# Denominators, output bias, shift products and weight folds moved to other steps of an adaLN block

## The chip, the cores and the metric

One core of a Trainium2 chip runs the whole kernel. The metric is the device time of one execution in microseconds (us). The kernel before took 342.48 us, the median of three runs (341.78 to 342.52).

## The reference

The input x is (2, 2048, 256) fp32: 2 batches, 2048 tokens each. From a conditioning vector six modulation rows per batch are made. Two residual branches follow, first a linear attention with 16 heads of 16, then 8 experts of which each token uses two.

```python
mod = (silu(c) @ wmod).reshape(B, 6, 1, E)      # sa, ca, ga, sb, cb, gb
ga, gb = sign * maximum(abs, 0.25)
h = layernorm(x) * (1 + ca) + sa
Q, K, V = h @ Wq.T + bq, h @ Wk.T + bk, h @ Wv.T + bv
Q, K = elu(Q) + 1, elu(K) + 1                   # per head
KV = einsum('bshd,bshe->bhde', K, V); K_sum = K.sum(over tokens)
Z = 1 / (einsum('bshd,bhd->bsh', Q, K_sum) + 1e-6)
x = x + ga * (einsum('bshd,bhde,bsh->bshe', Q, KV, Z) @ Wo.T + bo)
h = layernorm(x) * (1 + cb) + sb
gates = top-2 softmax(h/|h| @ (c/|c|).T + h @ w_route.T)
x = x + gb * sum_e gates[e] * (gelu(h @ w1[e] + b1[e]) @ w2[e] + b2[e])
```

## The kernel before

**Tiling.** The 4096 tokens are 32 tiles of 128, taken in 16 units of two tiles; units 0 to 7 are batch 0 and 8 to 15 batch 1. x and Q stay in on-chip memory as `x_sb` and `q_sb`, 32 tiles each. fp32 products are made as three passes of fp32r: each operand is split into a rounded high part (`_hi`) and the rest (`_lo`), and high times high, high times low and low times high are added (`mm3`, L983 to L985).

**Two pipelines.** Every engine runs its own program, `step_a(u)` for the attention of unit u = 0 to 15 and then `step_e(u)` for the experts, u = -1 to 15; semaphores tie them together. The order of calls in each step, written out by hand, is the order of the work on that engine, and an engine waits at the first call that is not ready. In this text "step n" is `step_a` of unit n and "expert step n" is `step_e` of unit n.

- In step u TensorE projects the unit's two tiles (`qk`), transposes the next unit (`tp_a`) and adds the previous unit's x^T K into a bank (`xk`). ScalarE makes exp(min(q, 0)) (`negative_part`, `exp_qk`), casts the next unit's transposed tile and normalises the unit after that (`normalise`). VectorE makes the low part of the next unit, then Q and K (`feature_map`) and statistics of later units. GpSimd makes rstd (`make_rstd`) and low parts.
- In expert step u TensorE makes both expert products of unit u (`first`, `second`), the transpose of q*z of unit u+3 (`tp_o`), its attention (`attend`), and of unit u+2 the transpose (`tp_e`) and the router product (`route`). VectorE makes gates (`gates_a`, `gates_b`), multiplies by them (`gate`), modulates, adds the attention and scales the experts. GpSimd makes q*z (`make_qz`), router norms (`norm_e`), low parts (`lo_e`) and the last addition.

**Shift product.** The shift sa would have to be added to every normalised tile. For units 0 to 2 ("plain") it is. From unit 3 on the scale is folded into the weights: `fold(b, c)` on VectorE (L1392) makes chunk c of batch b's folded Q and K weights from the raw weights, and the last feature, which the layernorm makes redundant, is replaced by the shift's own row. That row is sa times the raw weights plus the bias, made by the two fp32 products at L1128 (`c_sum`, kept by `keep_c`), and is put into row 127 of chunk 1 by a DMA, `put_rows(b)` (L394), which SP issues. ScalarE rounds the folded chunks (`cast_folded`, L758), GpSimd makes the low parts (`low_folded`, L513). Unit 3 waits for both chunks of batch 0, unit 8 for batch 1. Before the change SP issues batch 0's row behind the loads of units 4 and 5, batch 1's row behind the value weights (`wv_sb`, L415), the casts are in steps 1 and 5, and chunk 0 is done first.

**Values.** `value_constants` (L1068) multiplies the shift by the value weights, and waits for their DMA. `fold_values` (L1410) scales these weights; `kv_of(0, .)` in step 10 reads them.

**Denominators.** `make_prod(u)` on GpSimd (L578) multiplies Q by the sum of K into the single buffer `prod`; `denominators(u)` on VectorE (L1553) reduces it and takes the reciprocal z. `make_prod` of a unit waits until the denominators of the unit before are made. z of the first `Z_AHEAD` units goes to slots of their own (5 before), later ones share one. Units 0 to 4 are done in steps 10 to 15, unit u+5 in expert step u. The product of unit 5 is placed on GpSimd between `make_qz` and `lo_gates` of expert step 0, its denominator at the end of that step on VectorE.

**Output bias.** `add_bo(u)` on GpSimd (L528) adds ga*bo to x of unit u, in the steps of `BO_STEPS` for the first units (6 of them), and in expert step u-5 for the rest. `add_attention(u)` waits for it.

Of the kernel before, what the change touches and what calls it, by code (L numbers as in the profile page):

```python
# [57 lines left out]
BO_STEPS = (6, 8, 8, 10, 14, 15)  # L58

def adaln_block(nc, x, wqkvT, rows, cols, woT, w1, w2, b2, cT, wmod, out):  # L60
# [13 lines left out]
    with ctx:  # L74
# [50 lines left out]
        Z_AHEAD = 5  # L125
# [28 lines left out]
        gate_sign, gate_abs, gate_size = (q_sb[0:64, 8 + k, :] for k in range(3))  # L154
# [60 lines left out]
        folded = [q_sb[:, 4:4 + NC * 2, :].rearrange("p (c k) e -> p c (k e)", c=NC), tr_f.rearrange("p h c n -> p h (c n)")]  # L215
# [149 lines left out]
        def _(sp):  # L365
# [28 lines left out]
            def put_rows(b):  # L394

                sp.wait_ge(c_kept, 1)
                sp.wait_ge(folded_made, NC * (b + 1))
                sp.dma_start(folded[b][P - 1:P, 1, :], c_sum[b:b + 1, :]).then_inc(d_fold[b], 16)

            for it in range(2, NU // 2):  # L400
                load_x(it, 0)
                load_x(it, 1)
                if it == 2:
                    put_rows(0)
# [11 lines left out]
            put_rows(1)  # L416
# [45 lines left out]
        def _(pool):  # L462
# [50 lines left out]
            def low_folded(b, c):  # L513

                pool.wait_ge(fold_hi, NC * b + c + 1)
# [19 lines left out]
            def step_a(u):  # L535
# [8 lines left out]
                if u.nth(1):  # L544
                    for c in range(NC):
                        low_folded(0, c)
                if u.nth(5):
                    for c in range(NC):
                        low_folded(1, c)
                if weights_ahead(u):  # L550
                    split_weights_lo(u.count(1, -2))
                if u.plus(-3):
                    split_weights_lo(u.count())
                if u.nth(UPB + 2):
# [8 lines left out]
                if any(u.nth(j) for j in range(UPB + 4, UPB + 7)):  # L563
                    make_prod(u.plus(-2 - UPB))
                for k, at in enumerate(BO_STEPS):
# [12 lines left out]
            def make_prod(u):  # L578

                if u.nth(5):  # L580
# [55 lines left out]
            def lo_gates(u):  # L636
# [5 lines left out]
                if u.plus(4) and u.plus(-1):  # L642
# [7 lines left out]
            def step_e(u):  # L650
# [12 lines left out]
                if u.plus(5) and u:  # L663
# [4 lines left out]
                if u and not u.nth(0) and not any(u.nth(j) for j in range(UPB + 3, NU)):  # L668
# [27 lines left out]
        def _(act):  # L696
# [60 lines left out]

            def cast_folded(b, c):  # L758

                act.wait_ge(folded_made, NC * b + c + 1)  # L760
# [77 lines left out]
            def step_a(u):  # L838
# [9 lines left out]
                exp_qk(u, 0)  # L848
                if u.nth(NU - 1):
# [10 lines left out]
                if u.nth(1):  # L860
                    for c in range(NC):
# [3 lines left out]
                if u.nth(5):  # L865
                    for c in range(NC):
                        cast_folded(1, c)
                if u.nth(6):
                    scale_last_value_row()
# [976 lines left out]
```

## Time and profile before

| what | value |
|---|---|
| median of the runs | 342.48 us (341.78 to 342.52) |
| the profiled execution | 342.43 us |
| its span, first to last instruction | 340.7 us |
| TensorE matmul busy | 329.8 us, 97% of the span |
| TensorE weight load busy | 307.3 us, 90% |
| VectorE | 277.8 us, 82% |
| GpSimd | 235.2 us, 69% |
| ScalarE | 224.7 us, 66% |
| mean granted TensorE clock | 0.994 of 2.4 GHz |

Times in the trace are microseconds from the first instruction. PE is TensorE, DVE VectorE, ACT ScalarE, POOL GpSimd, SP SyncE; a "q" behind an engine's name marks its issuing of DMAs, and "bank" is an accumulation bank. A row "[1.09 <-ACT x L740]" means that the engine was idle for 1.09 us before this work, and that the result written at line 740 by ScalarE ended the wait. The attention steps run from about 9 to 103 us, the expert steps from there to the end, one about every 14.2 us once they are in their rhythm. A row with a colon in front, as 34.00:49.00, is a stretch: its length, then busy us (and instructions) of PE, PEld (the weight load), DVE, ACT and POOL, the granted clock, the DMA engines' busy share and GB/s. Matmuls overlap in the pipeline, so a matmul's own duration is longer than the distance to the next.

### The profile page before, as it was taken

The page shows a single profiled execution, that of the slowest core. Times are in us where ns is not written, and L with a number is a line of the kernel's source. Part 1 is how long each engine was busy: PE and PEld are TensorE (multiplying, and loading weights), DVE is VectorE, ACT ScalarE, POOL GpSimd, SP SyncE. Part 2 cuts the span into 40 slices and gives each one's busy share as a digit, 9 for nine tenths or more (in the row PEclk, how much of TensorE's full clock was granted, in tenths as well). Part 3 has the DMA queues.
Part 4 walks back from the last instruction along what each step waited for, and adds up shares of the span by engine and source line. Part 5 has one row for each costly group of instructions (what it writes and reads, how often), then busy time and mean ns, then how long its engine had stood idle before and what let it go on. Part 6 is the DMA issues. An engine that isn't in the chain of part 4 may idle for free.

```text
span 340.7 us, 7793 instructions
## 1 busy us (share of the span) xinstructions
PE 329.8 (97%) x2451; PEld 307.3 (90%) x2451; DVE 277.8 (82%) x788; ACT 224.7 (66%) x499; POOL 235.2 (69%) x335
## 2 busy tenths in 40 slices
PE   8999989999999978899999999999999999999996
PEld 8488858888879968899999999999999999999995
DVE  6588857796868889989898989899889897876864
ACT  4789769867676745585675857558576585765551
POOL 3467457657456587998987989888898876755210
PEclk9799999999999999999999999999999999999999
DMA  7976440000000321432324232232332423325221
GB/s 236 334 253 185 120 130 2 0 3 0 2 1 2 125 89 38 138 100 78 94 75 134 64 104 96 66 121 94 94 93 63 132 90 88 95 64 155 79 78 63
DMA packets 24271, 32.19 MB, mean 94 GB/s; under 512 B 2455, under 2 KB 14635, under 8 KB 24238
## 3 DMA queue, kind: packets, MB, share of 16 engines
q1 hardware_dynamic: 23796, 31.74, 30.3%
q8 instruction: 16, 0.26, 0.3%
q14 instruction: 17, 0.14, 0.1%
q10 hardware_dynamic: 442, 0.04, 0.1%
HBM read 27.43 MB, written 4.34 MB: 93 GB/s over the span
## 4 chain that ended last, share of the span: by engine, by line
PE 77%; DMA 10%; DVE 5%; SPq 4%; issue 1%; ACT 1%; POOL 1%; DVEq 0%; POOLq 0%; ACTq 0%
PE bank L983 21%; PE bank L984 21%; PE bank L985 21%; DMA x_sb<-in_x 7%; PE bank L1053 5%; PE bank L991 5%; PE bank L1211 2%; DMA early<-in_wqkvT 2%; PE bank L1253 1%; SPq L391 1%; DVE hid_g L1610 1%; SPq L390 1%; DMA mod_dram<-ksum_row 1%; DVE gT_f L1666 1%; PE bank L1064 1%
## 5 line engine op out<-in xcount | busy, mean ns | idle before, releaser
L919 ACT ACTIVATE bank<-bank,cols_sb 128x256 f32<-128x256 f32 x128 | 51.6, 440 | 47.9 <-PE bank L985 47.8
L983 PE MATMUL bank<-tr_hi,w_hi 128*128 128x256 f32 x256 | 72.7, 284 | 0.0
L983 PE MATMUL bank<-w_hi,hid_pair 128*128 128x256 f32 x256 | 71.8, 280 | 0.0
L984 PE MATMUL bank<-w_lo,hid_pair 128*128 128x256 f32 x256 | 71.6, 280 | 0.0
L985 PE MATMUL bank<-w_hi,hid_pair 128*128 128x256 f32 x256 | 71.6, 280 | 0.0
L985 PE MATMUL bank<-tr_hi,w_lo 128*128 128x256 f32 x256 | 71.5, 279 | 0.0
L984 PE MATMUL bank<-tr_lo,w_hi 128*128 128x256 f32 x256 | 71.5, 279 | 0.0
L620 POOL TENSOR_TENSOR hid_pair<-hid_g,hid_pair 128x512 fp32r<-128x512 f32 x42 | 55.0, 1310 | 4.0 <-ACT hid_pair L926 2.8
L983 PEld LDWEIGHTS bank<-w_hi,hid_pair 128*128 128x128 f32 x256 | 48.6, 190 | 0.0
L983 PEld LDWEIGHTS bank<-tr_hi,w_hi 128*128 128x128 f32 x256 | 48.5, 189 | 0.1
L984 PEld LDWEIGHTS bank<-tr_lo,w_hi 128*128 128x128 f32 x256 | 48.3, 189 | 0.0
L984 PEld LDWEIGHTS bank<-w_lo,hid_pair 128*128 128x128 f32 x256 | 48.2, 188 | 0.0
L985 PEld LDWEIGHTS bank<-w_hi,hid_pair 128*128 128x128 f32 x256 | 48.1, 188 | 0.0
L985 PEld LDWEIGHTS bank<-tr_hi,w_lo 128*128 128x128 f32 x256 | 48.1, 188 | 0.0
L926 ACT ACTIVATE hid_pair<-hid_g 128x512 fp32r<-128x512 f32 x48 | 30.2, 632 | 15.5 <-DVE hid_g L1610 15.0
L1610 DVE TENSOR_TENSOR hid_g<-bank,g_bc 128x512 f32<-128x512 f32 x48 | 33.0, 690 | 2.0 <-ACT bank L919 0.7
L1053 PE MATMUL bank<-k_sb,nat 128*128 128x256 f32 x128 | 30.2, 379 | 0.0
L774 ACT ACTIVATE e_sb<-bank 128x512 f32<-128x512 f32 x32 | 19.0, 595 | 14.9 <-PE bank L985 12.4
L983 PE MATMUL bank<-hid_pair,tr_hi 128*128 128x512 f32 x62 | 28.3, 457 | 0.4 <-DVE k_sb L1515 0.4
L1053 PEld LDWEIGHTS bank<-k_sb,nat 128*128 128x128 f32 x128 | 24.1, 189 | 3.7
L634 POOL TENSOR_TENSOR x_sb<-x_sb,k_sb 128x512 f32<-128x512 f32 (+1 forms) x15 | 19.5, 1301 | 10.3 <-DVE k_sb L1674 10.1
L492 POOL TENSOR_TENSOR rstd<-var_eps,minus_half 128x2 f32<-128x2 f32 (+1 forms) x28 | 22.2, 793 | 5.4 <-DVE var_eps L1371 3.2
(192 smaller groups left out, 858.6 us busy)
## 6 DMA issues: line engine op xcount, KB each, us to landing
g_bc<-g_dram SPq DMA_DIRECT2D x64, 256.0 KB, 3.5
x_sb<-in_x SPq DMA_DIRECT2D x16, 256.0 KB, 2.9
out<-x_sb SPq DMA_DIRECT2D x15, 256.0 KB, 2.3
early<-in_wmod SPq DMA_DIRECT2D x3, 512.0 KB, 7.5
q_sb<-in_w SPq DMA_DIRECT2D x2, 512.0 KB, 8.6
q_sb<-in_w SPq DMA_DIRECT2D x1, 1024.0 KB, 9.9
mod_row<-mod_dram SPq DMA_DIRECT2D x1, 1024.0 KB, 5.9
q_sb<-in_wqkvT SPq DMA_DIRECT2D x2, 256.0 KB, 5.2
```

The lines of the kernel that those rows point to most:

```text
L492: gp.tensor_tensor(rstd[:, of, :], var_eps[:, of, :], halves, ALU.pow).then_inc(power, 1)
L620: gp.tensor_tensor(hid_lo[:, p, :, :], hid_g[:, p % 2, :, :], hid_hi[:, p, :, :].bitcast(F32), ALU.subtract).then_inc(e_hlo, 1)
L634: gp.tensor_tensor(xt, xt, y_g[:, :, :], ALU.add).then_inc(e_y, 1)
L774: ac.activation(e_sb[:, t, :], bank[2 + t][:, :], ACT.Relu, scale=-1.0).then_inc(a_neg, 1)
L919: last = ac.activation(half, half, ACT.Gelu, bias=b1_sb[:, e:e + 1])
L926: ac.activation(hid_hi[:, p, :, :].rearrange("p j n -> p (j n)"), gated(p), ACT.Copy).then_inc(e_hhi, 1)
L983: te.matmul(out_ap, l_hi, r_hi, start=start, stop=False, skip_group_check=shared)
L984: te.matmul(out_ap, l_hi, r_lo, start=False, stop=False, skip_group_check=shared)
L985: return te.matmul(out_ap, l_lo, r_hi, start=False, stop=stop, skip_group_check=shared)
L991: last = te.transpose(dst[:, c, t * P:(t + 1) * P], of[:, t, c * P:(c + 1) * P], ident[:, :])
L1053: last = te.matmul(xk_bank(b)[:, c * E:(c + 1) * E], nat[:, slot_of(u), t, c * P:(c + 1) * P], k_sb[:, u.h, t, :], start=(first_of_batch a ...
L1610: TT(gated(p), bank[2 + p][:, :], g_bc[:, p, :, :].rearrange("p j n -> p (j n)"), ALU.mult).then_inc(e_mul, 1)
```

## The change

It moves calls between steps, reverses the order of the two folded chunks, and moves buffers so that the new order has room:

- `BO_STEPS` gets eight entries: units 0 to 7 in steps 6 to 13. The expert steps start with unit 8.
- `Z_AHEAD` is 7. `make_prod` of units 5 and 6 and their denominators are called in step 15; the denominators of unit 4 at the end of step 14, where they were at the start of step 15. The expert steps make products and denominators from unit 7 on.
- TensorE makes chunk 1 of the shift product behind the projection of unit 0; VectorE keeps the sum behind step 0.
- Folds, casts and low parts take chunk 1 first. Batch 0's low parts are made in GpSimd's step 2 (they were in 1). Of batch 1, chunk 1 is folded in step 4, chunk 0 in 5; cast in 5 and 6; both low parts are made in step 6.
- The row for the folded weights is issued by ScalarE (`put_row`) in steps 1 and 5, behind the first `exp_qk`; SP has no such DMA.
- The value constants are in step 7 (were in 6), the folded value weights in 8 (7), the centroid clip in 5 (4).

```diff
-BO_STEPS = (6, 8, 8, 10, 14, 15)
+BO_STEPS = (6, 7, 8, 9, 10, 11, 12, 13)
...
-        Z_AHEAD = 5
+        Z_AHEAD = 7
...
-        gate_sign, gate_abs, gate_size = (q_sb[0:64, 8 + k, :] for k in range(3))
+        gate_sign, gate_abs, gate_size = (early[0:64, (6 + k) * E:(7 + k) * E] for k in range(3))
...
-        folded = [q_sb[:, 4:4 + NC * 2, :].rearrange(...), tr_f.rearrange(...)]
+        folded = [q_sb[:, 6:6 + NC * 2, :].rearrange(...), tr_f.rearrange(...)]
...  # SP: put_rows and its two calls are gone
...  # GpSimd, step_a
-                if u.nth(1):
-                    for c in range(NC):
+                if u.nth(2):
+                    for c in reversed(range(NC)):
                         low_folded(0, c)
-                if u.nth(5):
-                    for c in range(NC):
-                        low_folded(1, c)
+                if u.nth(6):
+                    low_folded(1, 1)
...
+                if u.nth(6):
+                    low_folded(1, 0)
...
-                if any(u.nth(j) for j in range(UPB + 4, UPB + 7)):
+                if any(u.nth(j) for j in range(UPB + 4, UPB + 8)):
                     make_prod(u.plus(-2 - UPB))
+                if u.nth(NU - 1):
+                    make_prod(unit(6))
...  # GpSimd, lo_gates and step_e
-                if u.plus(4) and u.plus(-1):
+                if u.plus(4) and u.plus(-3):
                     wait(pool, o_prod, u.count(1, 5))
...
-                if u.plus(5) and u:
+                if u.plus(5) and u.plus(-2):
                     make_prod(u.plus(5))
...
-                if u and not u.nth(0) and not any(u.nth(j) for j in range(UPB + 3, NU)):
+                if u.plus(-3) and not any(u.nth(j) for j in range(UPB + 3, NU)):
                     add_bo(u.plus(UPB - 3))
...  # ScalarE
+            def put_row(b):
+                act.wait_ge(c_kept, 1)
+                act.wait_ge(folded_made, NC * b + 1)
+                act.dma_start(folded[b][P - 1:P, 1, :], c_sum[b:b + 1, :]).then_inc(d_fold[b], 16)
...
                 exp_qk(u, 0)
+                if u.nth(1):
+                    put_row(0)
+                if u.nth(5):
+                    put_row(1)
...
                 if u.nth(1):
-                    for c in range(NC):
+                    for c in reversed(range(NC)):
                         cast_folded(0, c)
...
                 if u.nth(5):
-                    for c in range(NC):
-                        cast_folded(1, c)
+                    cast_folded(1, 1)
                 if u.nth(6):
+                    cast_folded(1, 0)
+                if u.nth(7):
                     scale_last_value_row()
...  # TensorE
-                if u.nth(6):
+                if u.nth(7):
                     value_constants()
...
+            constants(0)
...
             step_a(u0)
+            constants(1).then_inc(c_made, 1)
             mod_rows()
...  # VectorE, feature_map
-                    if u.nth(2):
+                    if u.nth(3):
                         dve.wait_ge(fold_lo, NC)
...  # VectorE, step_e and step_a
-                if u.plus(5) and not u.nth(-1):
+                if u.plus(5) and u.plus(-2):
                     denominators(u.plus(5))
...
-                if any(u.nth(j) for j in range(UPB + 5, UPB + 8)):
+                if any(u.nth(j) for j in range(UPB + 5, UPB + 7)):
                     denominators(u.plus(-3 - UPB))
...
                 if u.nth(NU - 1):
                     lo_e(unit(0))
                     add_attention(unit(1))
+                    denominators(unit(5))
                 feature_map(u, 1)
+                if u.nth(NU - 1):
+                    denominators(unit(6))
...
                 if u.nth(UPB + 6):
                     lo_o(unit(1))
                     modulate_e(unit(0))
+                    denominators(unit(4))
...  # VectorE, between the steps
-            keep_c()
             for u in range(NU):
                 step_a(unit(u))
                 if u == 0:
-                    for c in range(NC):
+                    keep_c()
+                    for c in reversed(range(NC)):
                         fold(0, c)
                 if u == 4:
-                    for c in range(NC):
-                        fold(1, c)
-                if u == 6:
+                    fold(1, 1)
+                if u == 5:
+                    fold(1, 0)
+                if u == 7:
                     keep_value_constants()
-                if u == 7:
+                if u == 8:
                     for b in range(B):
                         fold_values(b)
...
-                if u == 4:
+                if u == 5:
                     clip_centroids()
```

## Rows read from the trace of the kernel before

**Rows 1.** Stretches: length, busy PE, PEld, DVE, ACT, POOL, clock, DMA share, GB/s.

```profile
8.70:12.10 3.40, 3.40 (x6) 0.38 (x6) 1.96 (x9) 2.79 (x7) 1.58 (x3) 0.53 1.03 371
...
34.00:49.00 15.00, 13.78 (x68) 10.49 (x67) 10.58 (x35) 10.76 (x22) 6.54 (x12) 1.00 0.48 142
...
116.10:138.30 22.20, 17.69 (x144) 16.48 (x143) 20.04 (x63) 13.51 (x34) 17.62 (x24) 1.00 0.21 73
...
141.50:325.00 183.50, 183.46 (x1573) 182.75 (x1571) 159.47 (x453) 117.28 (x280) 145.88 (x189) 1.00 0.32 96
```

**Rows 2.** TensorE's waits: for whom, us in total, times, longest.

```profile
PE bank L991 <- DVE x_sb L1574: 2.1, 2, 1.7
```

**Rows 3.** Timeline of TensorE, steps 1 and 3: start, us, what.

```profile
17.20 0.50 PE L983 MATMUL bank<-hid_pair,tr_hi 128*128 128x512 f32 x1
...
27.95 0.58 PE L983 MATMUL bank<-hid_pair,tr_hi 128*128 128x512 f32 x1
```

**Rows 4.** Timeline of GpSimd, steps 0 to 2.

```profile
16.40 1.43 POOL L510 TENSOR_TENSOR tr_lo<-tr_f,tr_hi 128x256 fp32r<-128x256 f32 x2
...
24.03 2.54 POOL L516 TENSOR_TENSOR hid_pair<-q_sb,hid_pair 128x512 fp32r<-128x512 f32 x2 [0.97 <-ACT hid_pair L764]
...
26.65 0.23 POOL L489 TENSOR_SCALAR neg_mean<-mv 128x2 f32<-128x2 f32 x1
...
28.05 0.20 POOL L494 TENSOR_TENSOR neg_mr<-neg_mean,rstd 128x2 f32<-128x2 f32 x1
```

**Rows 5.** Timeline of VectorE, unit 4's statistics, folds of batch 1.

```profile
24.00 0.25 DVE L1359 BATCH_NORM_AGGREGATE mv<-stats 128x2 f32<-128x6 f32 x2
...
40.95 1.39 DVE L1397 SCALAR_TENSOR_TENSOR tr_f<-q_sb,mod_col,early 128x512 f32<-128x512 f32 x2
```

**Rows 6.** Timeline of TensorE, steps 5 and 6.

```profile
41.76 1.89 PE L1053 MATMUL bank<-k_sb,nat 128*128 128x256 f32 x8
...
44.02 0.47 PE L983 MATMUL bank<-hid_pair,tr_hi 128*128 128x512 f32 x1 [0.38 <-DVE k_sb L1515]
...
45.50 0.60 PE L991 MATMUL bank<-ident,nat 128*128 128x128 f32 x4
...
46.94 1.02 PE L1074 MATMUL bank<-early,mod_col 128*2 128x256 f32 x4 [0.84 <-DMA early<-in_wqkvT]
```

**Rows 7.** DMA issues: queue, count, KB each, us from issue to landing.

```profile
c_sb<-in_cT ACTq DMA_DIRECT2D x1, 2.0 KB, 3.0
...
q_sb<-nat_e SPq DMA_DIRECT2D x1, 2.0 KB, 3.5
...
tr_f<-nat_e SPq DMA_DIRECT2D x1, 2.0 KB, 4.7
```

**Rows 8.** Timeline of ScalarE, step 5's second cast.

```profile
47.13 0.63 ACT L764 ACTIVATE hid_pair<-tr_f 128x512 fp32r<-128x512 f32 x1 [2.42 <-issue]
```

**Rows 9.** Timeline of GpSimd, steps 13 and 15.

```profile
87.45 0.75 POOL L525 TENSOR_TENSOR w_lo<-q_sb,w_hi 128x256 fp32r<-128x256 f32 x1 [3.20 <-DVE w_hi L1523]
...
101.22 1.28 POOL L532 TENSOR_TENSOR x_sb<-x_sb,mod_row 128x512 f32<-128x512 f32 x1
...
103.58 1.06 POOL L596 TENSOR_TENSOR early<-q_sb,early 128x512 f32<-128x512 f32 x1
```

**Rows 10.** Timeline of VectorE, gates of unit 0, a denominator, what follows.

```profile
103.83 1.07 DVE L1627 STREAM_TRANSPOSE bank<-bank 32x64 f32<-32x64 f32 x4
...
127.93 0.71 DVE L1558 TENSOR_REDUCE den<-early 128x32 f32<-128x544 f32 x1
...
128.94 1.02 DVE L1627 STREAM_TRANSPOSE bank<-bank 32x64 f32<-32x64 f32 x4
```

**Rows 11.** Timeline of TensorE, expert steps -1 and 1.

```profile
106.60 0.60 PE L991 MATMUL bank<-ident,early 128*128 128x128 f32 x4
...
115.63 0.31 PE L1211 MATMUL bank<-tr_hi,route_r 128*32 128x256 f32 x1 [0.16 <-DVE tr_lo L1595]
...
138.32 0.36 PE L1253 MATMUL bank<-b_r,gT_r 128*128 128x256 f32 x1 [0.57 <-DVE k_sb L1674]
```

More of the change, by code:

```diff
@@ L214, in adaln_block @@
         g_dram = nc.dram_tensor("g_dram", (2, NE, 2 * P), F32, kind="Internal").ap()
-        folded = [q_sb[:, 4:4 + NC * 2, :].rearrange("p (c k) e -> p c (k e)", c=NC), tr_f.rearrange("p h c n -> p h (c n)")]
+        folded = [q_sb[:, 6:6 + NC * 2, :].rearrange("p (c k) e -> p c (k e)", c=NC), tr_f.rearrange("p h c n -> p h (c n)")]
         c_sum = nat_e[0:B, :, :].rearrange("p t e -> p (t e)")
@@ L392, in _ @@
             sp.dma_start(wo_sb[:, :, :], woT.rearrange("(c p) n -> p c n", p=P)).then_inc(d_wo, 16)
[L394 to L398, printed above, removed]
             for it in range(2, NU // 2):
@@ L402, in _ @@
                 load_x(it, 1)
-                if it == 2:
-                    put_rows(0)
             sp.wait_ge(bo_ready, 1)
@@ L415, in _ @@
             sp.dma_start(wv_sb, wqkvT[:, 2 * E:3 * E].rearrange("(c p) n -> p c n", p=P)).then_inc(d_wv, 16)
-            put_rows(1)
             sp.wait_ge(cv_kept, 1)
@@ L513, in low_folded @@
             def low_folded(b, c):
-                pool.wait_ge(fold_hi, NC * b + c + 1)
+                pool.wait_ge(fold_hi, NC * b + 1 + (NC - 1 - c))
                 gp.tensor_tensor(fold_parts[b][1][:, c, :], folded[b][:, c, :], fold_parts[b][0][:, c, :].bitcast(F32),
@@ L578, in make_prod @@
             def make_prod(u):
-                if u.nth(5):
+                if u.nth(7):
                     pool.wait_ge(f_ksrow, B)
@@ L756, in scale_last_value_row @@
                 last.then_inc(v_row, 1)
+            def put_row(b):
+                act.wait_ge(c_kept, 1)
+                act.wait_ge(folded_made, NC * b + 1)
+                act.dma_start(folded[b][P - 1:P, 1, :], c_sum[b:b + 1, :]).then_inc(d_fold[b], 16)
             def cast_folded(b, c):
-                act.wait_ge(folded_made, NC * b + c + 1)
+                act.wait_ge(folded_made, NC * b + 1 + (NC - 1 - c))
                 if c == NC - 1:
@@ L1086, in step_a @@
                     tp_a(u.plus(1))
-                if u.nth(6):
+                if u.nth(7):
                     value_constants()
@@ L1125, in _, with constants @@
             te.matmul(bank[7][:, 0:B], last_feature(P), mod_col[:, 3, :], start=True, stop=True).then_inc(scale_made, 1)
-            for c in range(NC):
+            def constants(c):
                 pe.wait_ge(d_qk[c], 16)
-                last = te.matmul(bank[1][0:B, :], mod_col[:, c, :], wqk_raw[:, c, :], start=(c == 0), stop=(c == NC - 1))
-            last.then_inc(c_made, 1)
+                return te.matmul(bank[1][0:B, :], mod_col[:, c, :], wqk_raw[:, c, :], start=(c == 0), stop=(c == NC - 1))
+            constants(0)
             def mod_rows():
@@ L1782, in _ @@
                 if u == 0:
-                    for c in range(NC):
+                    keep_c()
+                    for c in reversed(range(NC)):
                         fold(0, c)
                 if u == 4:
-                    for c in range(NC):
-                        fold(1, c)
-                if u == 6:
+                    fold(1, 1)
+                if u == 5:
+                    fold(1, 0)
+                if u == 7:
                     keep_value_constants()
-                if u == 7:
+                if u == 8:
                     for b in range(B):
```

## The prediction

> **What bounds the kernel now.** I read the busy time by stage first [rows 1]. In that view the reader is to compare TensorE's busy time with each stage's length. From 141.5 to 325 us TensorE is busy 183.46 of 183.50 us: nothing done on another engine can shorten that stretch. It idles in two places that the change touches: 1.22 us between 34 and 49 us, and 4.51 us (22.20 - 17.69) between 116.1 and 138.3 us, where VectorE is busy 20.04 us. The list of waits, second [rows 2], has at its top whom TensorE waits for: VectorE's addition of the attention output to x (2.1 us in 2 waits). The timelines of the engines, third, give the places. So the sum has three terms: what the change does to TensorE at the start of attention (steps 0 to 3), at steps 5 and 6, and where attention hands over to the experts (steps 15, -1, 0, 1 of the two pipelines). Elsewhere I charge nothing, because TensorE runs without a gap there.
>
> **Steps 0 to 3.** The shift product (fp32, 2 output rows, two chunks) fills the stretch from 8.7 to 12.1 us, 3.4 us at a granted clock of 0.53 [rows 1], that is nearly all at 1.2 GHz of the levels 1.2 and 2.4. The second chunk moves behind the projection of unit 0. That projection could begin 1.7 us (half of 3.4) earlier, at 10.4. But TensorE's work up to unit 1 is the same, and unit 1's projection waits for GpSimd's low part of the transposed input, whose first half lands at 16.40 + 0.72 = 17.12 [rows 4]; it starts at 17.20 now [rows 3]. GpSimd begins it that late because it first makes rstd of unit 2, from statistics of an input tile that the DMA bounds. Value: 0. Bounds: -0.1 (nothing ahead of 17.12) and +0.9 (the moved half costs 0.85 us at the full clock and all of it is added).
>
> The low parts of the folded weights of batch 0 move from GpSimd's step 1 to step 2, behind rstd of unit 4. Now GpSimd does them at 24.03 to 26.57 (2 x 1.27) and then rstd, 26.65 to 28.25, 1.6 us [rows 4]. After: rstd can start when VectorE has unit 4's statistics, 24.00 + 0.25 = 24.25 [rows 5], and ends at 25.85 to 26.0; the two low parts end at 28.5. TensorE's projection of unit 3 needs both, and starts at 27.95 now [rows 3]. It slips by 0.55 to 0.85 us; I take 0.7. Bounds: 0 (if statistics and rstd run ahead of this) and +1.2: the row's DMA, discussed below, is issued at about 21.2 and takes the longest time of such a row, 4.7 us [rows 7]; the first cast then ends at 26.55 and the low parts at 29.1.
>
> **Steps 5 and 6.** Three things. First, VectorE's two folds of batch 1, 1.39 us together [rows 5], stand ahead of the feature map of unit 5, which TensorE waits for: unit 6's projection starts at 44.02 [rows 6], while the eight products in front of it begin at 41.76 and take 1.55 us to the next start where nothing is waited for (an estimate from their 1.89 us, the last 0.35 of which overlap what follows). That is 43.3, so 0.7 us is lost. With one fold there, VectorE is 0.7 us earlier (the centroid clip, 0.1, leaves too). TensorE now arrives 0.7 later by the slip above. The two meet: -0.7 of this loss pays for +0.7 of the slip, sum 0.0. Second, the product with the value weights moves from step 6 to step 7. TensorE stands from 45.50 + 0.36 = 45.86 to 46.94 for that DMA [rows 6]; a step later (about 50) it has landed. -1.1 us; the product's own 1.4 us only moves. In steps 7 and 8 TensorE's starts lag by 0.1 us each, since GpSimd is late with rstd behind the folds: -0.2, an estimate from the lengths of the steps around. Third, the DMA of the row for the folded weights moves from SP's queue to ScalarE's. In SP's queue it stood between x loads and behind the value weights; for SP its loss from the queue is worth nothing, since the x loads behind it wait for the x loads before them, and it was the last but the value rows. Queued behind ScalarE's issue are the second Relu of the same step, the Exp, and the next normalisation. The issue can run beside the Exp before it, and its wait on the fold is met at about 42.3 in step 5: I charge 0.
>
> What hangs on this DMA is when it lands. ScalarE's cast of that chunk now comes first of the two. In the trace it took 3.5 us (batch 0) and 4.7 us (batch 1) from issue [rows 7], and in batch 1 the cast waited 2.42 us for it [rows 8]. ScalarE's own first load, also 2 KB and beside SP's first loads, took 3.0 us [rows 7], and I take that. From an issue at 42.3 it lands at 45.3, half a us after ScalarE is free of normalisation, and the feature map of unit 6 is written at 48.7, still ahead of 48.85, when TensorE is due at unit 7's projection: no stall. With 4.7 us it lands at 47.0: the Relu of unit 6 starts 2 us late and unit 7's projection finds its bank free at 50.4. That costs 1.5 us. I take 0 and keep +1.5 as the bound. The Trainium skill bears on this ("DMA: Bandwidth & Descriptors", Queues, rings and completion order): each DMA engine goes round the queue rows that have work, a packet at a time. By that rule a row in ScalarE's own queue need not stand behind the value weights in SP's, and the sum stays as it is; by the two durations of 3.5 and 4.7 it would be 1.5 us worse. No row here shows a ScalarE DMA beside a long SP queue at that time.
>
> Steps 0 to 8 together: 0 + 0.7 - 0.7 - 1.1 - 0.2 = -1.3 us.
>
> **The output bias and the other sums.** Each addition is 1.28 us of GpSimd [rows 9]. Units 6 and 7 leave the expert steps 1 and 2 for attention steps 12 and 13; units 1, 3, 4 and 5 go one to four steps earlier. GpSimd idles 3.2 us in one gap ahead of step 13's weight split [rows 9], and gaps like it stand in the steps around, so all are hidden: 0. Without that cover each would put 1.28 us ahead of the rstd of its step.
>
> **The hand-over.** A denominator (reduction and reciprocal) takes VectorE 1.01 us, from 127.93 until its next work at 128.94 [rows 10]. Two of them (units 5, 6) leave expert steps 0 and 1 for attention step 15, and so do two products of 1.28 us on GpSimd. The one of unit 4 stays where it was, since the end of step 14 is the start of step 15. In step 15 they do not run in free time. GpSimd multiplies for unit 5 at 101.22 to 102.5 (in the bias addition's place [rows 9]); VectorE reduces at 103.17 to 104.2; only then may GpSimd multiply for unit 6, to 105.5; behind that in GpSimd's order stand the router's norm and then q*z of unit 2, which now ends at 103.58 + 1.06 = 104.64 [rows 9] and will end at about 107.55 (105.5 + 1.0 + 1.06). TensorE transposes it at 106.60 [rows 11]: +0.95 us of stall. VectorE reduces unit 6 to 106.55, so the gate logic of unit 0 starts at 106.55 and not 103.83 [rows 10], +2.7; statistics and rstd of unit 1 follow, and ScalarE's normalisation of it starts at about 111.3, 1.9 later. Behind it on ScalarE are two GELUs, the gates' casts, the squares and the cast of unit 1, and this brings TensorE's router product of unit 1, at 115.63 now [rows 11], to 117.1: +1.45.
>
> From there the rows of before hold, shifted by 1.45, down to the end of step 0, where the denominator is gone: 1.45 - 1.01 = +0.44. VectorE fills expert step 1 almost without a gap to its scaling of unit 0's experts, for which TensorE waits at 138.32 [rows 11]. Unit 6's denominator stood behind that point and gives nothing back: TensorE is the bound from there on. So the hand-over costs +0.45. Bounds: -2.0 (both denominators come off, the delay in step 15 vanishes in idle time) and +1.5 (the delay stays and nothing comes off).
>
> **Sum.** -1.3 + 0.45 = -0.85 us against the profiled execution, whose time is 342.43 us (span 340.7 and 1.7 around it); the median of the runs is 342.48, so both agree. Forecast: 341.6 us.
>
> **Rivals.**
> A. The hand-over gains: the delay in step 15 is caught up in VectorE's and ScalarE's idle time, and in expert steps 0 and 1 both VectorE's 1.0 us and GpSimd's 2.6 us (two products) count. For: 4.5 us of TensorE idle in that stretch. Against: the second reduction gives nothing before 138.32, so at most 1.0 from VectorE and an estimated 0.5 from GpSimd. 342.4 - 1.3 - 1.5 = 339.6.
> B. The low folded weights are later than I think. If GpSimd reaches them 0.6 later, unit 3 slips 1.3, of which step 5 gives back 0.7, and the hand-over stays at +0.45 to +1.0: 342.4 - 0.7 + 0.7 = 342.4, no change.
> C. Slower. The row DMA lands as late as in the trace, 4.7 us: ScalarE holds the Relu of unit 6 and TensorE loses 1.5 us at unit 7's projection, more than the 1.1 won. It decides from a landing later than about 45.5, 3.2 us after issue; with the hand-over between 0.45 and 1.45 that is 342.4 - 0.85 + 1.5 = 343.1 to 344.1.
> D. The change does not do what it says: step 15's denominators wait on GpSimd and all of the hand-over's cost stays (+1.5) while the early part gains: 342.4 - 1.3 + 1.5 = 342.6, again no change.
>
> **How the numbers follow.** My forecast holds 0.40, A 0.18, B 0.14, C 0.18, D 0.10. A difference below 0.2% (0.7 us) can't be told from none. The forecast's own spread is 0.7, so I count a fifth of it as falling within 0.2%; with A that makes faster 0.50, B, D and that fifth same 0.32, C slower 0.18. The range 339.7 to 343.4 leaves out a part of A at its low end and of C at its high end.
>
> **What would show it.** Right: TensorE stands 0.5 to 0.9 us ahead of unit 3's projection, no idle at the value product, the next chunk's cast on ScalarE without a DMA wait, then in the hand-over the transpose of unit 2's q*z about 1 us late, and a gap before unit 1's router product that shrinks by one denominator. Wrong: a ScalarE wait of 2 us in step 5, or a hand-over that ends earlier than before against the start of step 15.

## The result and the profile after

The changed kernel is slower, by 0.4%. Its median is 344.13 us (343.77 to 345.51, 10 runs) beside 342.67 us for the kernel before in the same session (341.78 to 343.38, 10 runs): ratio 1.0041, 95% interval 1.0022 to 1.0060. Forecast were 341.6 us and a range up to 343.4, so the time lies above the range, on the side of rival C (slower). The profiled execution took 344.18 us with a span of 342.5, against 342.43 and 340.7: +1.8 us to explain.

First the stretches of the kernel after, with the columns of [rows 1]. The last two are the stretches of before, taken 1.3 and 1.8 us later, because the expert steps start and run later by about that much.

```profile
8.70:12.10 3.40, 3.40 (x9) 1.50 (x9) 2.10 (x10) 2.79 (x7) 1.55 (x3) 0.57 1.03 375
34.00:49.00 15.00, 14.85 (x72) 12.12 (x70) 10.71 (x37) 10.82 (x22) 8.06 (x17) 1.00 0.47 141
...
117.40:139.60 22.20, 18.55 (x148) 16.92 (x146) 19.97 (x61) 13.76 (x34) 16.19 (x26) 1.00 0.28 92
143.30:326.80 183.50, 183.47 (x1573) 182.76 (x1572) 159.09 (x451) 117.38 (x280) 143.20 (x185) 1.00 0.32 96
```

From 143.3 on TensorE is busy 183.47 of 183.50 us, as before: nothing of the difference is there. Between 34 and 49 us TensorE idles 0.15 us, not 1.22, as the change meant; the idle time comes just behind. So the loss stands elsewhere, and the list of TensorE's waits (for whom, us in total, times, longest) names it:

```profile
PE bank L988 <- DVE k_sb L1523: 2.2, 2, 1.4
PE bank L996 <- DVE x_sb L1582: 1.6, 2, 1.2
PE bank L988 <- DVE qz_lo L1573: 1.4, 3, 0.8
...
PE bank L996 <- POOL early L590: 0.9, 1, 0.9
```

On top is now the feature map (`k_sb`), twice, and the last line is GpSimd's q*z, which was not waited for at all. TensorE's timeline (start, us, what) gives their places:

```profile
28.31 0.47 PE L988 MATMUL bank<-hid_pair,tr_hi 128*128 128x512 f32 x1
...
43.53 0.59 PE L988 MATMUL bank<-hid_pair,tr_hi 128*128 128x512 f32 x1
...
46.96 1.89 PE L1058 MATMUL bank<-k_sb,nat 128*128 128x256 f32 x8
50.22 0.47 PE L988 MATMUL bank<-hid_pair,tr_hi 128*128 128x512 f32 x1 [1.37 <-DVE k_sb L1523]
...
68.18 0.47 PE L988 MATMUL bank<-hid_pair,tr_hi 128*128 128x512 f32 x1 [0.81 <-DVE k_sb L1523]
...
108.87 0.66 PE L996 MATMUL bank<-ident,early 128*128 128x128 f32 x4 [0.90 <-POOL early L590]
...
117.95 0.31 PE L1219 MATMUL bank<-tr_hi,route_r 128*32 128x256 f32 x1 [0.16 <-DVE tr_lo L1603]
```

These are the projections of units 3, 6, 7 and 10, the transpose of unit 2's q*z and the router product of unit 1. Followed from one to the next, the kernel after stands against the kernel before as follows:

| start of | before | after | difference |
|---|---|---|---|
| projection of unit 3 | 27.95 | 28.31 | +0.36 |
| of unit 4 | 33.47 | 33.70 | +0.23 |
| of unit 6 | 44.02 | 43.53 | -0.49 |
| of unit 7, second tile | 53.46 | 53.62 | +0.16 |
| of unit 9 | 61.68 | 61.63 | -0.05 |
| of unit 10 | 66.95 | 68.18 | +1.23 |
| router product, unit 0 | 102.86 | 103.91 | +1.05 |
| unit 1 | 115.63 | 117.95 | +2.32 |
| unit 2 | 127.30 | 129.83 | +2.53 |
| unit 3 | 141.37 | 143.10 | +1.73 |

Two single steps lose more than the whole difference: unit 7 and unit 10.

**Unit 7.** The eight products ahead of it begin at 46.96, and the next start could be 1.54 us behind, as at 41.99 to 43.53. It is at 50.22: 1.72 us lost. (The row says 1.37, because it counts from the modelled end of the products, the last 0.35 us of which overlap what follows.) The prediction had priced this stall at 1.5 us for a row that lands after 4.7 us. Back from there, on ScalarE's timeline, then the DMA (us from issue to landing) and what SP issued ahead of it:

```profile
42.01 0.52 ACTq L756 DMA_DIRECT2D tr_f<-nat_e  x1
...
43.74 1.08 ACT L715 ACTIVATE nat<-x_sb,neg_mr,rstd 128x255 f32<-128x255 f32 x2
46.80 0.63 ACT L764 ACTIVATE hid_pair<-tr_f 128x512 fp32r<-128x512 f32 x1 [1.97 <-DVE tr_f L1405]
```

```profile
tr_f<-nat_e ACTq DMA_DIRECT2D x1, 2.0 KB, 4.7
```

```profile
40.28 0.38 SPq L406 DMA_DIRECT2D mod_row<-mod_dram  x1
40.71 0.47 SPq L407 DMA_DIRECT2D early<-in_wqkvT  x1
```

The row is issued at 42.01 and lands 4.7 us later, at 46.7; the cast of the folded chunk starts at 46.80. (The profile puts the wait down to the fold, which had long been done; the DMA came last.) This is the ScalarE wait of 2 us in step 5 that the prediction had named as a sign of being wrong. Behind that cast on ScalarE stand unit 6's first Relu and the cast of unit 7's transposed tile, and from there the delay goes over VectorE's low part and feature map to TensorE:

```profile
48.12 0.57 ACT L734 ACTIVATE tr_hi<-bank 128x512 fp32r<-128x512 f32 x1
```

```profile
48.72 0.69 DVE L1397 TENSOR_TENSOR tr_lo<-bank,tr_hi 128x512 fp32r<-128x512 f32 x1 [2.16 <-ACT tr_hi L734]
...
49.66 0.41 DVE L1523 SCALAR_TENSOR_TENSOR k_sb<-bank,e_sb 128x256 f32<-128x256 f32 x1
```

Ahead of the row, 1.3 to 1.7 us earlier, SP issued the modulation rows to all partitions (`mod_row`, 1 MB) and the value weights (`early`, 256 KB). The value weights took 5.8 us and landed at 46.5, so the row landed as they did.

**Unit 10.** VectorE, then GpSimd, in step 8:

```profile
63.30 2.90 DVE L1422 SCALAR_TENSOR_TENSOR early<-early,mod_col 128x256 f32<-128x256 f32 x4
...
66.68 0.69 DVE L1397 TENSOR_TENSOR tr_lo<-bank,tr_hi 128x512 fp32r<-128x512 f32 x1
```

```profile
63.66 1.47 POOL L523 TENSOR_TENSOR x_sb<-x_sb,mod_row 128x512 f32<-128x512 f32 x1
```

The four folds of the value weights took 1.64 us before, in step 7, each 0.45 to 0.48. Now they take 2.90: the shortest 0.47, the middle of them 0.57, the longest 1.51. The second of them would start at about 63.7, when GpSimd's bias addition starts (63.66 to 65.13), which is an entry of `BO_STEPS` that the kernel before does not have. The low part and the feature map of unit 9 come behind them, and TensorE loses 1.2 us at 68.18 (from the second tile of unit 9 to unit 10 it is 68.18 - 63.91 = 4.27 us, before 3.10). In the stretch from 60 to 70 us it had no idle time before (first row) and has 0.81 us now (second):

```profile
60.00:70.00 10.00, 10.00 (x54) 8.42 (x53) 7.91 (x24) 8.38 (x17) 7.58 (x11) 1.00 0.01 3
```

```profile
60.00:70.00 10.00, 9.19 (x46) 7.46 (x45) 9.42 (x25) 7.60 (x16) 8.00 (x13) 1.00 0.01 2
```

**The hand-over.** GpSimd, then VectorE:

```profile
105.40 1.28 POOL L580 TENSOR_TENSOR early<-q_sb,ksum_row 128x512 f32<-128x512 f32 x1 [1.83 <-DVE early L1568]
...
107.76 1.06 POOL L590 TENSOR_TENSOR early<-q_sb,early 128x512 f32<-128x512 f32 x1
```

```profile
106.71 0.72 DVE L1566 TENSOR_REDUCE den<-early 128x32 f32<-128x544 f32 x1 [0.79 <-POOL early L580]
...
107.74 1.02 DVE L1635 STREAM_TRANSPOSE bank<-bank 32x64 f32<-32x64 f32 x4
```

This is the order that the prediction had: GpSimd waits 1.83 us for the reduction of unit 5 before it may multiply for unit 6, q*z of unit 2 ends at 108.82, and the gates of unit 0 start at 107.74. From the first router product to the fourth it is 39.19 us, before 38.51: +0.68.

### The profile page after: what moved, and what is told of

It reads as the page before. It is cut to its first block, busy times and chain, and to the rows that moved or that the text cites. A ratio compares the mean times of both kernels' runs of the same rounds, so it can differ in the third digit from the quotient of the medians.

```text
span 342.5 us, 7791 instructions
## 1 busy us (share of the span) xinstructions
PE 329.8 (96%) x2451; PEld 307.6 (90%) x2451; DVE 279.0 (81%) x788; ACT 224.2 (65%) x499; POOL 236.8 (69%) x335
## 4 chain that ended last, share of the span: by engine, by line
PE 77%; DVE 11%; DMA 4%; issue 3%; ACT 2%; POOL 2%; SPq 1%; ACTq 0%; DVEq 0%; POOLq 0%
PE bank L988 21%; PE bank L989 21%; PE bank L990 21%; PE bank L1058 5%; PE bank L996 5%; DMA x_sb<-in_x 2%; PE bank L1219 2%; DMA g_bc<-g_dram 1%; PE bank L1261 1%; DVE gT_f L1674 1%; DVE stats L1361 1%; DVE hid_g L1618 1%; DVE bank L1635 1%; DVE den L1566 1%; DVE x_sb L1582 1%
```

## The experiments

Every kernel below was timed in five rounds beside the kernel before, whose medians in the three sessions were 342.81, 342.50 and 342.83 us. "First to fourth" is TensorE's time from the router product of unit 0 to that of unit 3.

**1. The loads.** The value weights go ahead of the modulation rows, and the rows' 1 MB broadcast waits until the folded row of batch 1 has landed.

```diff
+            sp.dma_start(wv_sb, wqkvT[:, 2 * E:3 * E]...)
             for g, k in enumerate(MOD_ROWS):
...
             sp.wait_ge(mod_put, 16 * len(MOD_ROWS))
+            sp.wait_ge(d_fold[1], 16)
             sp.dma_start(mod_row[:, :, 0:4, :], mod_dram[:, 0:4, :].partition_broadcast(P))
-            sp.dma_start(wv_sb, wqkvT[:, 2 * E:3 * E]...)
```

> The changed kernel, but SP issues the value weights before the modulation rows, and the 1 MB broadcast of the modulation only after the row for batch 1's folded weights has landed. Theory (the row lands 4.7 us after its issue because it shares the DMA engines with these two loads, and this holds ScalarE): the row lands 2 to 3 us after its issue, ScalarE's cast of chunk 1 waits less than 0.3 us instead of 1.97, TensorE's 1.37 us wait at unit 7's projection goes, the time falls by 1.1 to 1.4 us against the changed kernel, to 0.999 to 1.001 of the kernel before. Rival (a row of this shape takes 4 to 5 us from ScalarE whatever else moves): landing stays over 4 us, and the time stays at 1.004.

Measured: ratio 0.9989 (0.9972 to 1.0006), 342.43 us. ScalarE's timeline and the DMA of this kernel:

```profile
44.99 0.61 ACT L765 ACTIVATE hid_pair<-tr_f 128x512 fp32r<-128x512 f32 x1
```

```profile
tr_f<-nat_e ACTq DMA_DIRECT2D x1, 2.0 KB, 1.7
```

Same queue, same issuing engine, same bytes: 1.7 us in place of 4.7. The cast follows the normalisation without a wait; the second tile of unit 7 starts at 52.61 (after 53.62, before 53.46). The wait of 0.81 at unit 10 stays, with folds of 2.90 us. The intervals of this kernel and of the changed one don't touch. Which of the two loads held the row was not tried by itself.

The loss at unit 7 falls from 1.72 to 0.44 us and not to nothing (TensorE, then GpSimd, then VectorE):

```profile
47.23 1.89 PE L1059 MATMUL bank<-k_sb,nat 128*128 128x256 f32 x8
49.21 0.47 PE L989 MATMUL bank<-hid_pair,tr_hi 128*128 128x512 f32 x1
```

```profile
45.68 1.29 POOL L508 TENSOR_TENSOR hid_pair<-tr_f,hid_pair 128x512 fp32r<-128x512 f32 x1 [0.45 <-ACT hid_pair L765]
```

```profile
45.82 1.71 DVE L1406 SCALAR_TENSOR_TENSOR tr_f<-q_sb,mod_col,early 128x512 f32<-128x512 f32 x1
```

With the row on time, GpSimd makes the low part of chunk 1 just when VectorE folds chunk 0. That fold takes 1.71 us, where it takes 0.73 in the changed kernel, and VectorE works from it to the feature map without a gap. All five kernels that join the changed folds with the value weights first show this (1.70 or 1.71 us).

**2. The queue.** The other reading of the late row is ScalarE's queue. Here SP issues it, behind the value weights.

```diff
-                if u.nth(5):
-                    put_row(1)
...
             sp.dma_start(wv_sb, wqkvT[:, 2 * E:3 * E]...)
+            sp.wait_ge(c_kept, 1)
+            sp.wait_ge(folded_made, NC + 1)
+            sp.dma_start(folded[1][P - 1:P, 1, :], c_sum[1:2, :])...
```

> The changed kernel, but batch 1's row for the folded weights is issued by SP behind the value weights, as before the change, and not by ScalarE. Theory (the row is late because of what the DMA engines still carry, whichever queue it is in): it lands 4 to 5.5 us after its issue, TensorE's wait at unit 7's projection is 1.2 to 2.4 us as with ScalarE's queue, time 1.003 to 1.005. Rival (ScalarE's queue makes it later or sooner): the landing moves by over 1 us one way, and the time with it.

Measured: 1.0075 (1.0048 to 1.0102), 344.76 us. The DMA, then TensorE's start of unit 7:

```profile
tr_f<-nat_e SPq DMA_DIRECT2D x1, 2.0 KB, 5.2
```

```profile
50.50 0.47 PE L989 MATMUL bank<-hid_pair,tr_hi 128*128 128x512 f32 x1 [1.85 <-DVE k_sb L1524]
```

The row is late from SP's queue too. It is not the issuing engine that makes it late, but what is in flight. The Trainium skill states this ("DMA: Bandwidth & Descriptors", Issuing engines are not separate DMA queues): transfers started by either engine run on the same DMA engines and mix there. The two landings, 4.7 us from ScalarE and 5.2 from SP, agree. The time is above the 1.003 to 1.005 that were expected; in the profiled execution (345.41 us) TensorE's granted clock fell behind this stall (see the last section), which may be a part of it.

**3. The value folds.** `fold_values` back behind step 7, nothing else undone.

```diff
                 if u == 7:
                     keep_value_constants()
-                if u == 8:
                     for b in range(B):
                         fold_values(b)
```

> The changed kernel, but VectorE folds the value weights at the end of step 7, right behind keeping the value constants, and not after step 8. Theory (the fold, 2.9 us in step 8, ends after ScalarE has unit 10's cast ready, so VectorE is late with unit 9's feature map and TensorE waits 0.81 us at unit 10's projection): that wait goes, the four folds take 1.6 to 2.0 us, and the time falls by 0.8 to 1.0 us, to about 1.001 of the kernel before. Rival (step 7 has no more room than step 8): the wait moves to unit 9's projection and the time stays at 1.004.

Measured: 1.0036 (1.0013 to 1.0058), 343.64 us, not told apart from the changed kernel by time. By the trace the wait at unit 10 is gone (3.11 us from the second tile of unit 9) and the folds take 1.65 us. But the row landed only after 5.4 us here, TensorE waited 2.09 us at unit 7, and then something that no theory had (TensorE's granted clock is the number ahead of the last two):

```profile
50.00:51.00 1.00, 0.16 (x1) 0.20 (x2) 0.69 (x4) 0.97 (x3) 0.07 (x1) 1.00 0.00 0
51.00:52.00 1.00, 1.00 (x5) 0.77 (x5) 1.00 (x3) 1.00 (x3) 0.00 (x0) 0.89 0.00 0
52.00:53.00 1.00, 1.00 (x5) 0.70 (x4) 0.90 (x5) 0.79 (x3) 0.45 (x1) 0.50 0.00 0
53.00:54.00 1.00, 1.00 (x5) 0.48 (x4) 0.96 (x1) 0.74 (x2) 1.00 (x2) 0.50 0.00 0
```

TensorE fell to 1.2 GHz behind the stall. From the first to the second tile of unit 7 it is 4.99 us, in the changed kernel 3.40: 1.6 us more, which is more than the gain. This profiled execution took 344.98 us, 1.3 above the median, so most executions did not pay all of it; why their median is not at the expected 1.001 stays open.

**4. The bias addition.** The cause of the long fold is tested from the other side: the folds stay in step 8, on top of experiment 1, and the addition of step 9 goes to step 10.

```diff
-BO_STEPS = (6, 7, 8, 9, 10, 11, 12, 13)
+BO_STEPS = (6, 7, 8, 10, 10, 11, 12, 13)
```

> The kernel with the value weights loaded first (e1), and the output bias of unit 3 moved from step 9 to step 10, so that GpSimd adds nothing in step 9 before its rstd. The folds of the value weights stay behind step 8. Theory (a fold reads two operands of on-chip memory and waits while GpSimd's addition, which reads it too, holds the way to it): the slow fold of 1.5 us goes, the four take 1.65 to 2.1 us and not 2.90, TensorE's wait of 0.81 us at unit 10's projection falls under 0.3 us, the time by 0.5 to 0.9 us against e1, to 0.997. Rival (the fold is slow by itself there, or step 8 is full anyway): still 2.9 us and 0.999.

Measured: 0.9968 (0.9957 to 0.9980), 341.53 us. VectorE:

```profile
63.69 1.86 DVE L1423 SCALAR_TENSOR_TENSOR early<-early,mod_col 128x256 f32<-128x256 f32 x4
```

TensorE starts unit 10 without a wait, 3.24 us after the second tile of unit 9 (67.53 - 64.29; changed kernel 68.18 - 63.91 = 4.27, before 3.10). Of the 1.17 us lost there 0.14 are left: it was not the folds or their step that cost, but meeting the addition. The two times fit (342.43 us in experiment 1, 341.53 here), but their intervals overlap a little, so it is the trace that shows it.

**5. The hand-over.** Products and denominators of units 5 and 6 back in expert steps 0 and 1; then this together with 1 and 3.

```diff
-                if u.nth(NU - 1):
-                    make_prod(unit(6))
...
-                if u.plus(5) and u.plus(-2):
+                if u.plus(5) and not u.nth(-1):
                     denominators(u.plus(5))
...
-                    denominators(unit(5))
-                if u.nth(NU - 1):
-                    denominators(unit(6))
```

> The changed kernel, but the products and denominators of units 5 and 6 are back in expert steps 0 and 1; the output bias stays moved. Theory (in step 15 the two take a chain GpSimd, VectorE, GpSimd, VectorE that delays q*z of unit 2 and the gates of unit 0 by more than the one denominator gives back): from TensorE's first router product to its fourth it takes 38.5 us as before the change, not 39.2, and the time falls by 0.7 us to 1.002. Rival (the expert steps gain from the move, and the delay is from other shifted work): the stretch gets longer than 39.2 us and the time rises over 1.005.

Measured: 1.0031 (1.0006 to 1.0056), 343.70 us. First to fourth is 38.51 us again, exactly that of before. The row landed after 5.8 us here and the stall at unit 7 was 2.44 us, so the time shows little of it.

> The changed kernel with all three edits: value weights first, their fold at the end of step 7, units 5 and 6 back in the expert steps. Theory (three separate losses): the savings add, 2.6 to 3.1 us against the changed kernel, so the time is 0.995 to 0.997 of the kernel before. Rival (the stalls cover each other): less than 2 us comes off, and the time is 0.998 or more.

Measured: 0.9957 (0.9940 to 0.9975), 341.42 us; first to fourth 38.59. With the three causes gone the kernel is faster than before; how much of that belongs to the order of the loads, which is no part of the change, is the question of experiments 8 and 9.

**6. The hand-over alone.** The kernel before, with only the output bias, both denominators of step 15 and unit 4's denominator moved.

> The kernel before, with only the output bias and the hand-over of the change: eight output biases in steps 6 to 13, products and denominators of units 5 and 6 in step 15, denominator of unit 4 at the end of step 14. Theory (the hand-over costs by itself, whatever came ahead of it): unit 2's q*z is late again, TensorE's distance from the first to the fourth router product grows from 38.5 us to 39.2, and nothing changes ahead of step 14: ratio to the kernel before 1.002, about +0.7 us. Also: a bias addition in step 9 meets no weight fold there, since this kernel folds the value weights behind step 7, so unit 10's projection has no 0.8 us wait. Rival (the +0.7 came from the later start of the changed kernel and its shifted inputs): first to fourth stays at 38.5, ratio 1.000. Second rival (bias additions cost by themselves): step 9 shows the wait and the ratio is 1.004 or more.

Measured: 1.0007 (0.9990 to 1.0023), 343.25 us: no difference that can be measured, though the expected 1.002 lies in the interval too. First to fourth is 39.00 us, +0.49, so the mechanism is there whatever comes before it (TensorE waits 0.89 us for q*z at 108.27). The second rival is excluded: no wait at unit 10. It is about as large in the other kernels that have both units in step 15: 38.94, 38.89, 38.87 and 38.87 us in experiments 1, 3, 4 and 2, +0.36 to +0.43.

**7. Only unit 5.** As the kernel of all three, but unit 5 stays in step 15 and only unit 6 goes back.

```diff
-                if u.nth(NU - 1):
-                    make_prod(unit(6))
...
-                if u.plus(5) and u.plus(-2):
+                if u.plus(5) and u.plus(-1):
                     denominators(u.plus(5))
```

> The kernel with all three edits (e4), but unit 5's product and denominator are made in step 15, and unit 6's alone is back in expert step 1. Theory (the loss at the hand-over is the chain of two, product, denominator, product, denominator through the one buffer, in front of q*z of unit 2 and of the gates): with one, q*z of unit 2 is no later, TensorE has no wait for it, and the first to the fourth router product take 38.0 to 38.5 us against 38.6 in e4; time 0.995 to 0.996 of the kernel before. Rival (each denominator in step 15 costs its share): 38.9 us and 0.997.

Measured: 0.9948 (0.9931 to 0.9965), 340.58 us. GpSimd, then TensorE:

```profile
102.42 1.06 POOL L589 TENSOR_TENSOR early<-q_sb,early 128x512 f32<-128x512 f32 x1
```

```profile
105.59 0.60 PE L995 MATMUL bank<-ident,early 128*128 128x128 f32 x4
```

q*z of unit 2 ends at 103.48, two us ahead of its transpose, and first to fourth is 37.77 us: 0.74 less than before, and a little under the 38.0 to 38.5 expected. (By time alone this kernel can't be told from that of all three.) Unit 5's product on GpSimd takes the slot that the bias addition left; unit 6's was the one that had to wait for a reduction.

**8. The kernel before with the loads reordered.** Values first, row of batch 1 next, then the broadcast; all else as before.

> The kernel before with one edit on SP: value weights first, then the modulation rows, then batch 1's row for the folded weights, and only when this has landed the broadcast of the modulation. Nothing of the change. Theory (most of what the all-three kernel wins over the kernel before is this order of loads): TensorE's wait for the value weights and ScalarE's wait for the row go, 1.1 to 1.4 us less, 0.996 to 0.997 of the kernel before. Rival (it needs the reversed folds too): ScalarE still waits for the row and the gain stays under 0.5 us.

Measured: 0.9970 (0.9955 to 0.9985), 341.29 us. The row lands after 1.7 us (before 4.7), the wait for the value weights is gone. So the old kernel had a fault of the same kind, a load on which an engine waits behind the broadcast, and paid for it mostly at the value product and not at unit 7.

**9. What is left of the change.** The kernel of 8 with the output bias moved and unit 5 in step 15 (no moved folds, no split shift product), and beside it, on the same chip, kernel 7 again.

> The kernel before, with the three parts that gained: value weights loaded ahead of the modulation rows' broadcast and the row of batch 1 ahead of it too, eight output biases in steps 6 to 13, and unit 5 alone (not 6) in step 15. The shift product, the order of the folds and the low parts, and the value constants stay as before. Theory: values first gave -1.2 us (0.997), unit 5 alone gives -0.7 in the hand-over: 340.6 to 340.9 us, ratio 0.995. If the moved folds and shift product of the change are worth something by themselves beside these, the kernel with all of them and only unit 5 is faster than this one by 0.5 us or more; I expect the two within 0.5 us.

> The changed kernel with values first, folded value weights behind step 7, and unit 5 alone in step 15, once more, so that it stands beside the previous kernel on one chip. Expected 0.995 of the kernel before, as it was (0.9948). Theory: no difference from the previous kernel beyond 0.5 us. Rival (the moved folds gain by themselves): 0.5 to 1.0 us faster than it.

Measured: 340.73 us (340.30 to 341.44) and 340.90 us (340.52 to 341.22), both 0.9938 of before (0.9919 to 0.9957, and 0.9920 to 0.9957). The two can't be told apart by time: with the loads in order, no gain from the moved folds, low parts, value constants and shift product is seen. The traces say why. Against the first of the two kernels the second is 0.67 us later at unit 3 (most of it the low parts), 0.11 earlier at unit 6 (the split fold), 0.32 later at the second tile of unit 7 (the fold of 1.71 us beside the low part, as in experiment 1) and 0.58 later at unit 9. Either kernel beats both given ones.

## Why the prediction was wrong, step by step

- **Shift product: 0.** Right. Unit 1's projection starts at 16.96, before 17.20 [rows 3], and unit 2's at 22.48 against 22.53.
- **Low parts in step 2: +0.7.** Right in kind, a little too large. Against the start of unit 2 it slips 0.41 us in the changed kernel (5.83 us from unit 2 to 3, before 5.42), and 0.41 to 0.61 in the eight other kernels that have this move. Of this, +0.23 was left at unit 4.
- **Fold of batch 1 split: -0.7.** Right: from +0.23 at unit 4 to -0.49 at unit 6 is -0.72.
- **Value product a step later: -1.1.** Right. It runs at 52.23 with no wait, where TensorE stood from 45.86 to 46.94 before [rows 6].
- **Lag of steps 7 and 8: -0.2.** Right in size: from +0.16 at the second tile of unit 7 to -0.05 at unit 9. It goes with the value folds: from the second tile of unit 8 to unit 9 it takes 3.02 us in the changed kernel and 3.26 in experiment 3, which has them back behind step 7.
- **Landing of the row: 3.0 us taken, stall 0. This is the step that failed.** It lands after 4.7 us and costs 1.72; the bound was +1.5. The wait, its place and its path to unit 7 were drawn rightly in the prediction's second case. The value was taken from the nearest row by queue and size, ScalarE's own first load at 3.0 [rows 7]. The row that should have been taken was the one of the same transfer in the same place, 4.7 us, with SP's queue as the difference. Experiment 2 shows that the queue does not make it early (5.2 us from SP, 4.7 from ScalarE), experiment 1 that the 1.25 MB issued 1.3 to 1.7 us before it were the cause. The sentence on the round of the DMA engines over the queue rows pointed to an early landing; sharing by turns is no claim that a small transfer is quick while 1.25 MB pass, and I had read it as one.
- **"Elsewhere I charge nothing". This failed too.** The value folds were moved to step 8, the added bias addition to step 9, and each was costed alone, at nothing. They meet, and cost 1.17 us at unit 10. The reason given, that TensorE runs without a gap there, is true of the kernel before and no protection, as the two rows of the stretch from 60 to 70 us show. An engine that is never idle still stalls when what it needs next comes later. For the addition, idle time on GpSimd was looked for, not what VectorE does in it. No rival had this. The Trainium skill does ("SBUF — State Buffer", SBUF: two separate sides): a VectorE operation with two inputs in on-chip memory and a GpSimd operation that reads it hold a shared port exclusively, and the later one blocks. The traces agree: in the four kernels in which the addition meets the folds one fold takes 1.51 us and not 0.47, and in experiments 3 and 4, where they don't meet, the longest takes 0.47 and 0.68.
- **Hand-over: +0.45.** Right. 0.36 to 0.49 us in five kernels, 0.68 in the changed kernel's profile; what the other 0.2 are was not tried. Its terms were right too: q*z of unit 2 waited for 0.90 (0.95 forecast), router product of unit 1 later by 1.27 against the first (1.45), then a gain of 0.80 ahead of the fourth (1.01). What was not drawn from it is that the second of the two units makes the loss, and that the first alone would gain.

The sum as it should have stood: +0.23 - 0.72 - 1.08 + 1.72 = +0.15 at unit 7; -0.1 to the second tile of unit 9; +1.17 at unit 10; -0.18 from there to the first router product (the table's +1.23 and +1.05); +0.68 in the hand-over. That is +1.7 of the measured +1.8. The mechanism of rival C is the one that came true, and its chance of 0.18 was too low for a landing time that the trace had already shown once. That 344.1 us is also the upper end of rival C is luck: it gets there with a hand-over of 1.45, which measured 0.68, and without the step of unit 10, which it did not have.

## What to carry to other kernels

A small DMA on which an engine waits is priced by what is in flight at its issue, and not by which engine issues it; put it ahead of the bulk load, or make the bulk load wait for it (-1.2 us in experiment 8). When a GpSimd operation is moved into free time, read what VectorE does in that stretch: two operations that each cost nothing can block each other, and a cured stall can bring the next pair together, as at unit 7 in experiment 1. An engine without idle time in a stretch is no reason to charge nothing there. When two items are moved into one gap, work out each by itself: here the first gains 0.7 us and the second loses more than that.

## What the runs showed of the hardware

- The same 2 KB transfer took 1.7 us in all seven profiles in which the broadcast stood behind it, and 4.7 to 5.8 us in the six in which it stood ahead (4.7, 4.7, 5.1, 5.2, 5.4, 5.8). In all six the row landed within 0.3 us of the value weights ahead of it: the time from issue is long where the broadcast was issued only 0.5 us before the row (5.8 us, experiment 5) and shorter where it was 1.7 or 2.0 us before (4.7). Batch 0's row, issued among the loads of x, took 1.9 to 4.1 us. The runs' times fit: experiment 3, with the stall, spreads from 343.09 to 346.64 us, experiment 1, without it, from 342.14 to 342.97.
- TensorE's clock can fall behind a stall of some 2 us. In experiments 2 and 3 the granted clock was 0.50 from 52 to 55 us, after waits of 1.85 and 2.09 us, and unit 7 took 1.6 us more; after the wait of 1.37 us in the changed kernel it stayed at 1.00, and after 2.44 us in experiment 5 as well. In those two executions the stretch from 8.7 to 12.1 us, which other work covers, had a clock of 1.00 in place of the 0.50 to 0.62 of the others (of the rest, only experiment 7's first kernel had 1.00 there as well, and it has no such stall). The length of the stall alone doesn't decide it; what does was not tried. A stall of this size therefore costs its own length in some executions and 1.6 us more in others.
- The blocking between GpSimd and VectorE is not tied to the value folds: a fold of batch 1 that takes 0.73 us elsewhere took 1.71 us in experiment 1, beside a low part on GpSimd (45.68 to 46.97), and cost TensorE 0.44 us.
